# A graph network on one core: gate expands issued before their sums, the edge layer's weighted sums written out straight, gated bias in whole banks, a bias on GpSimd, three clearings fewer

## Time and profile before

| | |
|---|---|
| runs | 7599.15, 7609.82, 7611.53 us |
| profiled execution | 7616.87 us, its span 7615.1 us, mean granted clock 0.779 |
| PE busy | 5623.5 us (74%) |
| DVE busy | 4161.0 us (55%) |
| POOL busy | 2913.2 us (38%) |
| ACT busy | 2234.0 us (29%) |

### The profile page before, as it was taken

How to read it: one execution, slowest core, us unless ns; L and a number is a source line. 1 busy time by engine, 2 the same in 40 slices (tenths; PEclk the granted TensorE clock), 3 DMA queues, 4 the chain that set the end, 5 groups by cost and what they waited for, 6 DMA issues and landing times. The chain is left out here.

```text
span 7615.1 us, 87812 instructions
## 1 busy us (share of the span) xinstructions
PE 5623.5 (74%) x21265; PEld 4036.6 (53%) x21266; DVE 4161.0 (55%) x8501; ACT 2234.0 (29%) x5333; POOL 2913.2 (38%) x2892
## 2 busy tenths in 40 slices
PE   1788679178867688668855666669989993565998
PEld 0566446156646466456643333337778882443676
DVE  4566623466653577747774555551257775775112
ACT  0333212133321333233323333322225551001333
POOL 1666232376600466356634555520027772000000
PEclk9666679566668666666666888879989996886999
DMA  3444133244410344334431111100049994331000
GB/s 83 129 115 116 35 112 101 72 122 116 113 24 2 106 115 116 80 114 116 114 73 29 22 22 22 22 6 17 6 160 352 355 339 98 120 121 17 17 12 21
DMA packets 455410, 710.55 MB, mean 93 GB/s; under 512 B 105113, under 2 KB 334038, under 8 KB 455014
## 3 DMA queue, kind: packets, MB, share of 16 engines
q0 software_dynamic: 142432, 380.88, 18.9%
q1 hardware_dynamic: 310442, 318.36, 13.3%
q10 hardware_dynamic: 2304, 8.52, 0.3%
HBM read 604.94 MB, written 102.97 MB: 93 GB/s over the span
## 5 line engine op out<-in xcount | busy, mean ns | idle before, releaser
L653 POOL DMA_INDIRECT l_edges_stage<-l_h_rows,src_t x832 | 831.5, 999 | 461.2 <-issue 238.2
L890 PE MATMUL l_edges_ps_sum<-l_edges_msg,l_edges_hot 128*128 128x264 f32 x1664 | 741.5, 610 | 171.9 <-DVE l_attn_acc L764 157.2
L2645 PE MATMUL l_gate_edges_ps<-l_gate_edges_wide,l_gate_edges_hot_lo 128*128 128x500 f32 x1024 | 591.9, 745 | 308.8 <-DVE l_gate_edges_wide L2574 308.8
L2512 POOL DMA_INDIRECT l_gate_edges_srow<-l_gate_src_rows,l_gate_edges_idx x512 | 567.6, 1109 | 566.1 <-DVE l_gate_edges_val L2568 267.0
L2076 POOL DMA_INDIRECT l_edge_kv<-l_kv_rows,src_t x416 | 463.6, 1114 | 791.5 <-POOLq L1989 606.6
L890 PEld LDWEIGHTS l_edges_ps_sum<-l_edges_msg,l_edges_hot 128*128 128x128 f32 x1664 | 447.5, 291 | 371.4 <-DVE l_attn_acc L764 275.4
L2645 PEld LDWEIGHTS l_gate_edges_ps<-l_gate_edges_wide,l_gate_edges_hot_lo 128*128 128x128 f32 x1024 | 246.6, 248 | 613.8 <-issue 529.3
L653 POOL DMA_INDIRECT l2b_edges_stage<-l2b_h_rows,src_t x416 | 413.6, 994 | 236.7 <-issue 116.3
L653 POOL DMA_INDIRECT l2a_edges_stage<-l2a_h_rows,src_t x416 | 412.5, 992 | 237.9 <-issue 116.0
L890 PE MATMUL l2b_edges_ps_sum<-l2b_edges_msg,l2b_edges_hot 128*128 128x272 f32 x832 | 355.8, 582 | 88.2 <-DVE l2b_attn_acc L764 80.0
L1136 PE MATMUL l_agg_ps<-l_agg_msg,l_agg_hot 128*128 128x264 f32 x832 | 273.5, 499 | 193.6 <-DVE l_attn_acc L1104 171.7
(11 more groups left out here) (745 smaller groups left out, 11536.2 us busy)
## 6 DMA issues: line engine op xcount, KB each, us to landing
l_val_rows<-l_edge_vj SPq DMA_DIRECT2D x104, 512.0 KB, 5.5
l_agg_stage<-l_val_rows SPq DMA_DIRECT2D x52, 1024.0 KB, 5.4
l_edge_ea<-in_edge_attr SPq DMA_DIRECT2D x388, 128.0 KB, 5.1
l_edges_rel_b<-rel_rows SPq DMA_DIRECT2D x52, 512.0 KB, 4.0
l_experts_w<-in_L_ffn_w SPq DMA_DIRECT2D x32, 512.0 KB, 4.8
l_gate_edges_lo_b<-l_gate_edges_lo_rows SPq DMA_DIRECT2D x64, 256.0 KB, 3.3
l_edges_stage<-l_h_rows,src_t POOLq DMA_INDIRECT x832, 2.8
l2a_edges_rel_b<-rel_rows SPq DMA_DIRECT2D x26, 512.0 KB, 4.0
```

Source lines behind the costliest of these rows:

```text
L653: nc.gpsimd.indirect_dma_start(out=stage[:, c % 2, u, :], out_offset=None, in_=h_rows, in_offset=bass.IndirectOffsetOnAxis(ap=K.src_t[:, c ...
L890: nc.tensor.matmul(ps_sum[u][:], hot[:, g, u, :], msg[:, g % 2, u, :], start=True, stop=True).then_inc(summed, 1)
L2512: nc.gpsimd.indirect_dma_start(out=srow[:, n % 4, u, :], out_offset=None, in_=src_rows, in_offset=bass.IndirectOffsetOnAxis(ap=idx[:, n * ...
L2645: nc.tensor.matmul(flat, hot_lo[:, n % 2, u, :], wide[:, n % 2, u].rearrange("p t f -> p (t f)"), start=False, stop=False).then_inc(summed, 1)
```

## The change

1. `gate_edges`: TensorE issues `expand(n + 2)` ahead of `sums(n)`; `hotT` has three slots, and ScalarE runs `straight(n + 1)`, then `turned(n + 3)`. `ad` and `picked` lie head by head, so that the reduction runs over neighbours.
2. `aggregate_values`: all 52 rounds are written out with constant addresses. ScalarE makes the one-hots (8 Abs and a Relu a round). Block numbers come from `block_ids`, every second round. GpSimd zeroes `accs[1]`, VectorE `accs[0]`. SP waits for `weighed`.
3. `gated_bias`: all transposes come first, four tiles to a bank, with one copy a bank; then the products, two tiles to a bank, with one add a bank. The transposes no longer wait for the bias.
4. `finish_gat`: in l2b GpSimd adds the bias to `out` (128x6400) while VectorE works on the sums; in l2a the bias is added into `out`, and the copy is left out.
5. `clear_semaphores` is no longer called ahead of the feed-forward parts of l0, l1 and l3.

```diff
 # aggregate_values
             def _(sp):
-                with sp.Fori(0, NB // SLOTS) as j:
...
+                for n in range(NB):
+                    if n >= SLOTS:
+                        sp.wait_ge(weighed, n - SLOTS + 1)
+                    sp.dma_start(stage[:, n % SLOTS], ...).then_inc(gathered[n % SLOTS], 16)
             def _(dve):
-                nc.vector.memset(accs[0], 0.0)
-                nc.vector.memset(accs[1], 0.0).then_inc(added, PSL)
-                def build(n, j, m):
...
+                nc.vector.memset(accs[0], 0.0).then_inc(zeroed, 1)
+                def weigh(n):
+                    dve.wait_ge(gathered[n % SLOTS], 16 * (n // SLOTS + 1))
+                    if n >= 2:
+                        dve.wait_ge(summed, (n - 1) * BATCH)
+                    nc.vector.tensor_tensor(msg[:, n % 2, :, 0:D]..., bcast(L[...], C), ALU.mult).then_inc(weighed, 1)
+                def add(n, ids):
+                    for u in range(BATCH):
...
+                        to = accs[u % 2][:, bass.ds(ids[n % 2 * BATCH + u], 1), :].rearrange("p a d -> p (a d)")
+                        nc.vector.tensor_tensor(to, to, ps[u][:], ALU.add).then_inc(added, 1)
+                weigh(0)
+                for n in range(NB):
+                    if n % 2 == 0:
+                        ids = block_ids(nc, mybir.EngineType.DVE, K, n // 2)
+                    if n + 1 < NB:
+                        weigh(n + 1)
+                    add(n, ids)
+            def _(pool):
+                nc.gpsimd.memset(accs[1], 0.0).then_inc(zeroed, 1)
             def _(act):
+                for n in range(NB):
+                    if n >= 2:
+                        act.wait_ge(summed, (n - 1) * BATCH)
+                    for u in range(BATCH):
+                        nc.scalar.activation(hot[:, n % 2, u, :], K.col[:], ACT.Abs, bias=K.nrel_t[...]).then_inc(near, 1)
+                    nc.scalar.copy(msg[:, n % 2, :, D:D + HEADS], L[...]).then_inc(w_placed, 1)
+                    act.wait_ge(near, (n + 1) * BATCH)
+                    nc.scalar.activation(hot[:, n % 2], hot[:, n % 2], ACT.Relu, bias=K.ones[:, 0:1], scale=-1.0).then_inc(hot_built, 1)
 # finish_gat
+            if bias is not None and add and not relu:
+                @block.gpsimd
+                def _(pool):
+                    pool.wait_ge(bias_in, 16)
+                    nc.gpsimd.tensor_tensor(out[:], out[:], b[:].unsqueeze(1).to_broadcast([P, NT, D]), ALU.add).then_inc(biased, 1)
-                if bias is not None:
+                if bias is not None and (relu or not add):
                     dve.wait_ge(bias_in, 16)
-                    ch.link(nc.vector.tensor_tensor(flat, flat, b..., ALU.add))
+                    ch.link(nc.vector.tensor_tensor(flat if relu else out[:], flat, b..., ALU.add))
...
-                else:
-                    ch.link(nc.vector.tensor_copy(out[:], flat))
 # gated_bias
+                for g, ts in enumerate(groups):
+                    for t in ts:
+                        last = nc.tensor.transpose(bank[g][0:E, ...], gates[:, t, :], K.ident[:])
+                    last.then_inc(turned, 1)
                 pe.wait_ge(b_in, 16)
...
+                for j, ts in enumerate(pairs):
+                    pe.wait_ge(kept, min(j, len(groups) - 1) + 1)
+                    if j >= len(bank):
+                        pe.wait_ge(added, j - len(bank) + 1)
+                    for t in ts:
+                        last = nc.tensor.matmul(bank[j % len(bank)][...], gT[:, t, :], b[:], start=True, stop=True)
+                    last.then_inc(made, 1)
 # gate_edges
-        ad = ph.sb("ad", [P, NT, GH])
+        ad = ph.sb("ad", [P, GH, NT])
-        hotT = ph.sb("hotT", [P, 2, GB * P])
+        hotT = ph.sb("hotT", [P, 3, GB * P])
-        picked = ph.sb("picked", [P, GB, NT, GH])
+        picked = ph.sb("picked", [P, GB, GH, NT])
-                    ch.link(nc.vector.tensor_reduce(a_d[:], picked[:].rearrange("p u t h -> p u h t"), AX.X, ALU.add))
+                    ch.link(nc.vector.tensor_reduce(a_d[:], picked[:], AX.X, ALU.add))
                 straight(0)
+                turned(2)
                 for n in range(NBG):
                     exps(n)
-                    if n + 2 < NBG:
-                        turned(n + 2)
                     if n + 1 < NBG:
                         straight(n + 1)
+                    if n + 3 < NBG:
+                        turned(n + 3)
 # TensorE
                 for n in range(NBG):
-                    sums(n)
                     if n + 2 < NBG:
                         expand(n + 2)
+                    sums(n)
 # gnn_moe_program, three times
-        clear_semaphores(nc)
```

More of the change, by code:

```diff
@@ L1066, in aggregate_values @@
         PSL = 8
-        claimed = ph.sem("claimed")
         ps = [ph.psum(f"ps{m}", [P, ROW]) for m in range(PSL)]
-        free, hot_built, w_placed, summed, added = (ph.sem(s) for s in ("free", "hot_built", "w_placed", "summed", "added"))
+        near, hot_built, weighed, w_placed, summed, zeroed, added = (ph.sem(s) for s in ("near", "hot_built", "weighed", "w_placed", "summed", "zeroed", "added"))
         gathered = [ph.sem(f"gathered{m}") for m in range(SLOTS)]
@@ L1073, in _ @@
             def _(sp):
-                with sp.Fori(0, NB // SLOTS) as j:
[L1075 to L1079, removed]
+                for n in range(NB):
+                    if n >= SLOTS:
+                        sp.wait_ge(weighed, n - SLOTS + 1)
+                    sp.dma_start(stage[:, n % SLOTS], edge_rows[n * BATCH:(n + 1) * BATCH].rearrange("s p d -> p s d")).then_inc(gathered[n % SLOTS], 16)
@@ L1125, in _ @@
             @block.tensor
             def _(pe):
[L1127 to L1136, removed]
+                for n in range(NB):
+                    pe.wait_ge(hot_built, n + 1)
+                    pe.wait_ge(weighed, n + 1)
+                    pe.wait_ge(w_placed, n + 1)
+                    for u in range(BATCH):
+                        q = n * BATCH + u
+                        if q >= PSL:
+                            pe.wait_ge(added, q - PSL + 1)
+                        nc.tensor.matmul(ps[u][:], hot[:, n % 2, u, :], msg[:, n % 2, u, :], start=True, stop=True).then_inc(summed, 1)
@@ L1398, in gated_bias @@
 def gated_bias(nc, K, name, gates, E, b2, acc, residual):
+    TG = 4
     with Phase(nc, name) as ph:
@@ L1425, in _ @@
             @block.scalar
             def _(act):
-                for t in range(NT):
-                    act.wait_ge(turned, t + 1)
-                    nc.scalar.copy(gT[:, t, :], psg[t % 4][:]).then_inc(kept, 1)
+                for g, ts in enumerate(groups):
+                    act.wait_ge(turned, g + 1)
+                    nc.scalar.copy(gT[:, ts[0]:ts[-1] + 1, :].rearrange("e t p -> e (t p)"), bank[g][0:E, 0:len(ts) * P]).then_inc(kept, 1)
             @block.vector
             def _(dve):
-                for t in range(NT):
-                    dve.wait_ge(made, t + 1)
+                for j, ts in enumerate(pairs):
+                    dve.wait_ge(made, j + 1)
+                    to = acc[:, ts[0]:ts[-1] + 1, :].rearrange("p t d -> p (t d)")
+                    frm = bank[j % len(bank)][:, 0:len(ts) * D]
```

78 lines of the change are left out of this document (32 added, 46 removed).

## The result

The changed kernel takes 7088.38 us (median of 4 runs, 7084.73 to 7092.03) against 7608.77 for the kernel before, run beside it: a ratio of 0.9318, with a 95% interval of 0.9302 to 0.9334. The forecast was 7105. The profiled execution took 7091.57 us with a span of 7089.8: 525.3 us less than the profiled one of before, where the terms summed to 505.

| part | forecast | measured | from |
|---|---|---|---|
| gate_edges | 279 | 284.8 | first gather to copy: 742.8 against 1027.6 us |
| weighted sums | 178 | 180.3 | VectorE's zeroing to the closing addition: 287.8 against 468.15 |
| gated bias, three | 30 | 41.7 | 24.4 against 38.3 us each |
| finish_gat | 12.7 | about 10 | l2a 6.8, l2b 3.3 |
| clearings | 5 | 3.8 | VectorE's waits at the starts of the parts |

What follows compares the result with a forecast made beforehand. No engine was busy all through, so stages were priced singly: 279 + 178 + 30 + 12.7 + 5 = 505 us off the profiled 7616.9 gives 7112, and 7105 for the median, 7.1 us lower. Range 7050 to 7225.

Steps and rivals of the forecast that it cites:

- The ring: gate_edges: expand, VectorE's chain and TensorE's sums run one after another, about 15.7 us a round; expanding first opens it.
- 11.3 us a round: gate_edges after the change: GpSimd becomes the bound with 8 gathers of 1.414 us a round; gain 279 us.
- I keep the mean: gate_edges: gathers stay at their mean of 1.114 us, since VectorE does the same two-input work a round.
- rival of contended gathers: gate_edges: most gathers take 1.46 us, 13 to 14.1 us a round; total 7214 to 7284 us; chance 0.09.
- lower bound: gate_edges: no gather slowed by the wide products, 8 x 1.24 = 9.9 us a round, gain 369 us.
- The low clock, 32 us: gate_edges: TensorE's granted clock falls in its idle time, making rounds 11.8 us, 32 us less gain.
- The clock rival: Weighted sums: TensorE stays at 1.2 GHz, 52 x 1.65 = 86 us more, total 7191 us; chance 0.09.
- 25 x 0.86: gated_bias: products of 25 tiles at 0.86 us each, at 1.2 GHz, within the forecast 28.3 us.
- Clock up in gated bias: Rival, gated_bias: clock at 2.4 GHz halves the products, 3 x 10.7 = 32 us less, total 7073; chance 0.06.
- slower: Rival, gate_edges: gathers slowed to 2.43 us each, pause included, cost more than all gains; chance 0.01, later 0.02.
- first list: Whole kernel: chances of forecast 0.70, contended gathers 0.09, TensorE low 0.09, clock up 0.06, expand without effect 0.05, slower 0.01.
- all but the last: Whole kernel: every listed case except slower makes the kernel faster; chance given as 0.97.

## Why the prediction was right, point by point

- **The ring and GpSimd as the next bound:** right, and shown. One reading of the ring was off: "Sums 9.3 to 9.9" leaves out the rounds of 8.45 and 8.50 us among those between 4400 and 4530; the forecast used the average of 15.7 us a round and doesn't hang on it. Undoing the order alone gave 248.6 us back where the ring without the 0.59 us of reduction gives 247. Taking gathers away shortened the stage, and VectorE's longer reduction did not lengthen it.
- **11.3 us a round:** right. "I keep the mean" held because VectorE's wide products cost the gathers 1.36 us a round however the two streams lie. The rival of contended gathers (13 to 14.1 us) failed there: it assumed that gathers slow down whenever VectorE is busy, but they do so beside the wide products, which fill 4.8 of 11.3 us. The lower bound (9.9 us, "which the wide products exclude") is what the kernel with `val` in PSUM reaches, 10.0. The 5.8 us above the forecast lie mostly in the tail: the copy starts 20.4 us behind the last gather's start, where the forecast had 24 (4787 to 4811).
- **The low clock, 32 us:** did not arise. Sums of 8.64 us do occur, but with GpSimd at 11.3 they fill time in which TensorE would be idle. My 9.9 + 1.9 = 11.8 took the worst round of the kernel before.
- **Weighted sums:** right, 180.3 against 178, and both parts of it by themselves. One of them was sized 12% high (one-hots, 1.09 and not 1.22), the loads 3% low. A round takes 5.43 us and not 5.35, as the load of 16 shows with 0.38 a round and not 0.28; that this didn't reach the sum is luck, as the 3 us set aside for a low clock at first were not needed. (TensorE's gap, put at about 1.7 us, is 5.35 - 3.83 = 1.5 by its own rows; 82.8/52 = 1.6 was measured.) The clock rival failed: the granted clock was 0.95 to 0.96, and TensorE took 409 ns a half against 499 before.
- **Gated bias:** mechanism right, size off: 13.9 each and not 10. The term "25 x 0.86" took the clock at 0.50 throughout; behind the transposes it was at 0.93 for 4 us. "Clock up in gated bias" came true for a part of the stretch. I had taken the low clock as it stood, without a cause; the rows of the operands are what it turned on.
- **finish_gat:** the overlap was sized at 1 us with 3 as its bound, and was 3.5: beside GpSimd's two-input addition VectorE's pass lost nearly all of the 3.66 us. GpSimd's addition itself took 13.65 us, inside my 7 to 14; my estimate from the Trainium skill (GPSIMD Engine Reference, Elementwise — side-by-side cycle accounting) was 14.
- **Clearings:** 3.8 and not 5; the boundary without one still shows 0.85 us, not 0.32.
- Together the misses are +5.8, +2.3, +11.7, -2.6 and -1.2: 16 of the 20 us between 505 and 525.3. The last 4 are in none of these stretches, and no more than whole times vary by.
- **The chances:** "slower" stands at 0.01 in the first list and at 0.02 in the second, and by the first list "all but the last" is 0.99 and not 0.97.

## What to carry to other kernels

When a ring of dependences is opened, the new period is the largest sum of work on one engine, and it can be read ahead from the rows; an edit's worth depends on that bound (the layout: nothing behind GpSimd's gathers, and some part of 36 us in the ring). A slowdown by a neighbour should be priced by the work that causes it, a fixed amount a round, not as a longer mean of the victim; here it went with one operand moved to PSUM. Before a pass is given to another engine, look for a wait on its own engine into which it fits.

## What the runs showed of the hardware

- A GpSimd gather of 0.94 us takes 1.17 to 1.47 beside VectorE's 128x500 products with both inputs in SBUF (the first of a round least), and no gather takes more than 1.01 with one of their inputs in PSUM, at the same VectorE time (675 and 669 ns). The delay is nearly one-sided there. Between two long two-input passes it is not: VectorE lost 3.5 us in a 3.7 us overlap with GpSimd's 128x6400 addition.
- TensorE fully busy with products of 8 rows was granted 0.50; after 25 transposes over 128 rows 0.93 for 4 us; with the same products padded to 128 rows 1.00 until they ended.
- One load of 16 numbers to registers every second round (1.10 us), in place of 8 single ones a round (0.30 us each), took VectorE's rounds from 7.75 to 5.43 us.
